# Two causal attentions: transpositions three units behind the scores in place of two, values and output projection one unit later

## The reference, cut to what matters

```python
# layer 1 (16 heads of 128, with biases)
logits = einsum('bthd,bThd->bhtT', q, k) / sqrt(128) - 1e10 * (1 - causal)
out = einsum('bhtT,bThd->bthd', softmax(logits), v).reshape(...) @ w_o + b_o
# layer 7 (16 heads of 128, ALiBi)
scores = clip(einsum('bqhd,bkhd->bhqk', q, k) / sqrt(128), -1024, 1024) + slopes * key + causal(-inf)
out = einsum('bqhd,ohd->bqo', einsum('bhqk,bkhd->bqhd', softmax(scores), v), Wo)
```

## Time and profile before

| | |
|---|---|
| median of 3 runs | 3634.22 us (3633.18 to 3634.63) |
| the profiled execution | 3630.22 us, its span 3628.0 us |
| PE busy | 3313.8 us, 91% |
| DVE busy | 2526.7 us, 70% |
| ACT busy | 2199.4 us, 61% |
| POOL busy | 951.1 us, 26% |
| granted TensorE clock, mean | 0.966 |

### The profile page before, as it was taken

How to read it: one execution, slowest core, us unless ns; L and a number is a source line. 1 busy time by engine, 2 the same in 40 slices (tenths; PEclk the granted TensorE clock), 3 DMA queues, 4 the chain that set the end, 5 groups by cost and what they waited for, 6 DMA issues and landing times. The chain is left out here.

```text
span 3628.0 us, 64882 instructions
## 1 busy us (share of the span) xinstructions
PE 3313.8 (91%) x25040; PEld 2512.6 (69%) x25052; DVE 2526.7 (70%) x4681; ACT 2199.4 (61%) x4437; POOL 951.1 (26%) x1089
## 2 busy tenths in 40 slices
PE   6999999999897959689999998697999999999979
PEld 6999999999784748222222223486898989888868
DVE  5777766666563346599999994346887878788843
ACT  5777777777651424258888886224676767676632
POOL 2333343232241014412222210302322232223200
PEclk9999999999998979879999999899999999999989
DMA  2010000000000100211111100201101010101010
GB/s 76 21 33 21 24 13 24 13 24 13 1 1 22 37 15 20 65 25 24 24 24 27 31 13 4 121 1 47 42 30 42 30 42 30 42 30 42 13 70 24
DMA packets 45055, 108.94 MB, mean 30 GB/s; under 512 B 20670, under 2 KB 29374, under 8 KB 37200
## 3 DMA queue, kind: packets, MB, share of 16 engines
q1 hardware_dynamic: 27664, 87.91, 7.1%
q0 software_dynamic: 17088, 16.89, 2.0%
HBM read 89.89 MB, written 14.42 MB: 29 GB/s over the span
## 5 line engine op out<-in xcount | busy, mean ns | idle before, releaser
L1621 ACT ACTIVATE ga5m_pr<-ga5m_E 128x512 f32<-128x512 f32 (+1 forms) x683 | 533.1, 811 | 170.9 <-PE ga5m_E L1579 157.6
L1638 DVE TENSOR_REDUCE ga5m_nm<-ga5m_M 128x1 f32<-128x1024 f32 x512 | 598.6, 1218 | 51.2 <-PE ga5m_M L1555 39.8
L371 POOL TENSOR_TENSOR all_X<-all_X,at_part 128x512 f32<-128x512 f32 x256 | 334.9, 1308 | 997.4 <-ACT at_part L554 997.3
L436 PE MATMUL at_A<-all_ident,at_prob 128*128 128x128 f32 x2304 | 340.6, 274 | 29.4 <-ACT at_prob L562 20.2
L1592 PE MATMUL ga5m_O<-ga5m_pr,ga_Vx 128*32 128x256 f32 x4096 | 324.9, 394 | 0.0
L436 PEld LDWEIGHTS at_A<-all_ident,at_prob 128*128 128x128 f32 x2304 | 265.2, 140 | 58.3 <-DVE at_q1l L636 24.8
L1579 PE MATMUL ga5m_E<-ga5m_Q,ga5m_K 51*128 51x512 bf16 x1024 | 270.5, 388 | 20.6 <-ACT ga5m_pr L1621 20.1
L1555 PE MATMUL ga5m_M<-ga5m_K,ga5m_Q 48*128 48x512 bf16 x1024 | 232.7, 398 | 47.5 <-DMA ga5m_Q<-ga_qs 27.5
L652 DVE TENSOR_TENSOR at_pT1l<-at_A,at_pT1h 128x512 fp32r<-128x512 f32 (+1 forms) x384 | 235.5, 641 | 57.6 <-ACT at_pT1h L543 51.1
L850 ACT ACTIVATE ff_sil<-ff_gate 128x512 f32<-128x512 f32 x128 | 76.6, 598 | 272.1 <-PE ff_up L768 272.1
L950 DVE TENSOR_TENSOR ff_hf<-ff_sil,ff_up 128x512 f32<-128x512 f32 x128 | 87.8, 686 | 220.0 <-ACT ff_sil L850 220.0
(11 more groups left out here) (385 smaller groups left out, 10006.3 us busy)
## 6 DMA issues: line engine op xcount, KB each, us to landing
at_raw<-in_pack SPq DMA_DIRECT2D x32, 1027.0 KB, 5.8
at_slope<-in_slopes SPq DMA_DIRECT2D x32, 512.0 KB, 4.1
ga5m_Q<-ga_qs POOLq DMA_DIRECT2D x32, 192.0 KB, 3.3
ga5m_Q<-ga_qs POOLq DMA_DIRECT2D x32, 128.0 KB, 3.5
ga_qs<-ga5r_part SPq DMA_DIRECT2D x24, 128.0 KB, 2.1
ga5m_Q<-ga5m_mpart SPq DMA_DIRECT2D x192, 2.0 KB
all_X<-in_x SPq DMA_DIRECT2D x1, 2048.0 KB, 7.1
at_traw<-in_gu SPq DMA_DIRECT2D x8, 256.0 KB, 2.6
```

The costliest lines, as they stand in the source:

```text
L371: nc.gpsimd.tensor_tensor(X[:, t:t + 2, :], X[:, t:t + 2, :], part[(i - 1) % 2][:, :, :], ALU.add).then_inc(added, 1)
L436: mm = nc.tensor.transpose(bank(x)[:, (kt % 4) * P:(kt % 4 + 1) * P], prob[u % 4][:, kt * P:(kt + 1) * P], consts["ident"][:, :])
L1621: nc.scalar.activation(pr[:, a % NR:a % NR + b - a, :].rearrange("p a n -> p (a n)"), Eb[:, a % 3:a % 3 + b - a, :].rearrange("p a n -> p ...
L1638: nc.vector.tensor_reduce(nm[h % 2][:, r:r + 1], src[:, :], AX.X, ALU.max, negate=True).then_inc(m_read, 1)
```

## The change

`turns` takes the unit U - 3 (`LAG`), so the transposes come one step later. "pv" and "o" change places between odd and even steps and come one step later, so they stay one step behind the second transpose that they need. They are put at the head of `others(U)` and no longer at its end: on every engine they come before the step's projections. One more step is run at the end.

```diff
+    LAG = 3
...
-            kind, g = ("pv", "o")[u % 2], (u - 4) // 2 % 4
-            at = n if u >= 4 else n - 1
+            kind, g = ("o", "pv")[u % 2], (u - 5) // 2 % 4
+            at = n if u >= 5 else n - 1
             if 0 <= at < NHALF:
-                out.append((kind, at, g))
+                out.insert(0, (kind, at, g))
             return out
...
-            n, u = divmod(U - 2, QT)
-            return [("t", U - 2, a) for a in range(u // 4 + 1)] if 0 <= U - 2 < NU else []
-
-        LAST = NU + 4
+            n, u = divmod(U - LAG, QT)
+            return [("t", U - LAG, a) for a in range(u // 4 + 1)] if 0 <= U - LAG < NU else []
+
+        LAST = NU + 5
```

## The result

The changed kernel takes 3770.96 us (median, 3766.72 to 3772.46), the kernel before in the same comparison 3634.43: a ratio of 1.0372 with a 95% interval of 1.0354 to 1.0390, slower. The prediction was 3782. The profiled execution has a span of 3764.6 us against 3628.0, 136.6 more. The bias attention's last matmul moves from 970.2 to 1013.6, so it costs 43; the ALiBi attention runs 1077 us in place of 982, 95 more; the six layers between and after are the same within 2 us.

The account below looks back on a forecast made before the run. PE's own work was taken to bound the bias attention, with room in the ALiBi attention. Bias 50, ALiBi 73 and 43, less 26, clock 8: +148 us, 3778 profiled, median 4.0 above, 3782; range 3670 to 3835.

Parts of the forecast that it names:

- The bias attention can only lose: Bias attention: PE is busy 398.06 of 400 us, so a new order can only add waits; 50 us over 31 heads.
- A: All heads: the second group of t6's transposes waits for a bank not yet taken out, delaying pv 2; 0.85 us.
- B: All heads: pv 3 waits for its transposes' low part, late on DVE; 0.75 us in bias, 1.35 in ALiBi attention.
- C: ALiBi attention: pv 1 waits for its transposes' low part, behind two DVE passes; 0.15 us, between 0 and 0.3.
- D: ALiBi attention, 15 even heads: o 2 waits because pv 2 is taken out behind ACT's split of the weights; 2.4 us.
- The second wait at pv 3: ALiBi attention, even heads, after o 2's wait: pv 3 waits 1.8 us for DVE, 0.5 more than B.
- What goes: ALiBi attention: 15 transpose waits for the exponential, 20.2 us, and most of 8.0 us of bank waits; 26 us taken.
- The sum: Whole kernel: added waits and clock loss less the waits that go, +148 us; chance 0.60.
- The smaller waits: Rival, both attentions: A and B at their lower ends of 0.3, C at 0, no clock loss; 3679, chance 0.18.
- The gain: Rival: DVE and ACT keep ahead of PE, so only the removal of waits is left; 3608, chance 0.11.
- the one wait for another: Rival: A and B hidden, D at 1.7 in place of 1.35 and the bank waits; 3634, chance 0.05.
- The clock in every head: Rival: each ALiBi head loses 1.5 us to a lower clock, 46 in place of 8; 3820, chance 0.06.

Follow-up runs that it names:

- exchanging DVE's two duties: The changed kernel with DVE taking out the low parts of the transposes ahead of the row minimum, not behind it: 3867.81 us, ratio 1.0647.
- the early weights: The next pair's weight load asked for one head earlier on SP: 3712.96 us in the changed kernel, 3605.42 us in the kernel before.

## Why the prediction was right

- *The bias attention can only lose.* Right: 43 us, 50 predicted. A + B was 1.60 a head; measured 30.40 - 28.60 = 1.80 in the second half, less in the first half, where a head took 29.1 to 30.0 before and takes 30.4 to 30.9. Why the first half loses less is open.
- *A.* 0.85 predicted, 1.0 by the starts in both attentions. In the ALiBi attention pv 2 comes 1.71 after t6 (2759.76 to 2761.47) in place of 0.70. In the bias attention it comes 1.28 after it (710.48 to 711.76), and S1 loses 0.36 more, which the prediction had named. The mechanism as told holds (t6's second group waits for the bank of t5's first, behind the longest exponential), and moving q to step 0 takes it away. I called it a term of pv 2; it belongs to the light step.
- *B.* Right. By the starts 0.79 in the bias attention (0.02 to 0.81), 0.75 predicted, and 1.38 in the other (0.02 to 1.40), 1.35 predicted; moving pv and o behind the projections takes it away. The count of DVE's queue was right to 0.2 us: t7's low part 3.54 after the end of q predicted, 718.70 - 715.36 = 3.34 measured, and pv 3 0.26 after it where I had allowed nothing. That exchanging DVE's two duties would help does not follow from it.
- *C.* Mis-sized: 0.15 predicted, at most 0.3. The bracket shows 0.23, but by the starts pv 1 comes 0.94 after t4 (2753.95 to 2754.89) where the bias attention has 0.46: 0.48 a head.
- *D.* The wait was right, its price too low. o 2 waits 1.65 to 3.4, 2.4 on average (33.0 / 14); predicted 2.4, but in 15 heads. The second wait at pv 3 is mostly 1.1 to 1.8 (1.85 predicted), but 0.4 to 0.8 where D is longest, since what runs between them then runs at 1.2 GHz. D with its clock is 58 us by the early weights; the prediction had 43 + 8.
- *What goes.* The 20.2 us went, as forecast, but the early weights take them away in the old order too, which nothing in the prediction said. The bank's waits of 8.0 us were sized by their brackets, at some 6 us or 0.2 a head; by the starts they were worth 0.59 a head, 18 us.
- *The sum.* +148 predicted, +136.6 in the profiled executions. Bias 43 against 50; ALiBi 95 against 98. The last is close in part by luck: A, B and C together are 2.87 us a head in place of 2.35, and the bank's wait that went with the old order 0.59 in place of 0.2. The two misses, 16 and 12 us, take most of each other away, and what is left, 2.28, is what an odd head grew by (31.5 less 29.2).
- *The rivals.* The smaller waits (3679) failed in A and B, which were at their upper values. The gain (3608) and the one wait for another (3634) failed because A and B were not hidden. The clock in every head (3820) failed too: with waits of up to 1.13 us only, all heads run at 1.00. The Trainium skill, "TensorE: Matmul & The Clock Gate", section "A second HAM failure mode: psum-queue depth-cycling", has the clock change to and fro in such a cycle of banks; here it fell only where the waits were long, at D, and the changed kernel with the early weights, which still waits up to 1.1 us in each head, kept 1.00. With waits of 2.15 us in every head, as when DVE's duties were exchanged, it was below 1.00 in all of them.

## What to carry to other kernels

A wait for an engine that works in program order is worth following to what stands ahead on that engine: here a transpose waited for an exponential, that for a split of weights, that for a DMA which the order of the SP queue held back, and moving that one load on the queue made the kernel 0.8% faster, where the new schedule made it 3.7% slower. Lengthening a pipeline by one step moves all other distances as well; count, for each pair of producer and user, the time that PE has left between them, and whether any step becomes too light to cover what the other engines take out of it. Before the gains of two edits are added up, see whether one of them puts work into the chain that another wait hangs on, as q's copies came between the split and o 2. And size a wait by the starts on both sides, in the old order too: there the bracket showed a third of what the bank's wait cost.

## What was not expected of the hardware

A wait's price on PE was larger than the idle time beside it: pv 3's bracket of 0.54 us goes with 0.79 by the starts, because the bracket begins at a modelled end. The granted clock was 0.95 in an even head with waits of 3.37 and 0.51 us, and 1.00 over stretches full of waits of up to 1.13 us.
